# Gaps to the running maxima in an RWKV mixing stage: two VectorE operations replaced by a second key projection and a matmul with a negative identity

## The chip, the cores and the metric

The kernel runs on one core of a Trainium2 chip. The metric is the device time of one execution in microseconds; an execution is launched once and computes the whole decoder layer. The engines are PE (TensorE), DVE (VectorE), ACT (ScalarE), POOL (GpSimd) and SP (SyncE, which only issues DMAs here). "PEld" is the weight load of a matmul.

## The reference

The layer is mixing (RWKV), cross attention, and an attention and mixture-of-experts block. Only the mixing stage changes. Its core, for 16 sequences of 128 steps and 256 channels, once forward and once backward in time:

```
r, k, v = x @ rkv_w.T            # per direction, 256 channels each
per step t, per channel:
    ku = k + u;  m = max(mx, ku)
    y  = (exp(mx-m)*num + exp(ku-m)*v) / (exp(mx-m)*den + exp(ku-m))
    mw = mx + w;  mn = max(mw, k)          # w = -exp(time_decay)
    num = exp(mw-mn)*num + exp(k-mn)*v
    den = exp(mw-mn)*den + exp(k-mn)
    mx  = mn
out = (sigmoid(r) * y) @ out_w.T ;  x = layernorm(x + out)
```

All four exponentials depend only on the difference of the key `k` and the running maximum before it, `mx`: they are `exp(-relu(...))` of plus or minus that difference and a number that is constant in a channel.

## The kernel before

The program is written by hand, engine by engine, with semaphores; no scheduler reorders it. The stages follow one another; the mixing stage runs roughly from 65 to 274 us of the profiled execution.

**Units.** Mixing works on 16 units: 4 groups of 4 sequences, and in each group 4 units of 128 channels (u = 0, 1 forward, u = 2, 3 backward). A unit is 128 partitions by 512 columns (4 sequences of 128 steps). Unit n has place u = n mod 4 in group n // 4. PSUM has three banks for even and three for odd units (receptance, key, value); two more banks hold the output rows of a group.

**What one unit passes through.** PE projects it (`project`, L488: six fp32 128x512 matmuls, which stand in the trace as 12 records). DVE makes the running maxima of the keys with four scans of 128 columns (L655) into `top`, then two gaps with `scalar_tensor_tensor` on the key bank and `top` (L664 and L666) into two of the four planes of `weight`. ACT makes all four planes from these with two Relu passes over 1024 columns (L585, L587), and one Exp over 2048 (L589). POOL multiplies values into them (`new_parts`, L609 and L611). DVE runs the two carry scans (L672, L675). POOL forms numerator and denominator (`add_old`, L620 twice, L623, L624). DVE divides (`finish`, L682, the reciprocal L685, L689) into `y`. After a group's four units PE adds the residual (`copy_rows`, L547, two matmuls) and the output projections (`project_out`, L553, one for each unit), and DVE normalises (`norm`, `norm_rows`).

**The order that is written out.** Step n of DVE is: carry scans of unit n; `gaps` of unit n+2; at u = 3 `norm_rows` of the group before; `finish` of unit n-1; at u = 2 `norm` of the group before. Ahead of `finish` it waits, at u = 1, 2 and 3 of every group but the first, until the output projection of unit n-4-1 has read `y` (`unit_joined` at n-4, L720). Step n of PE is: `project` of unit n+2; at u = 1 `copy_rows` and output projections 0 and 1 of the group before; at u = 2 its output projections 2 and 3. `project` of unit m waits only until unit m-2 has left its banks: values and gates copied by ACT (`vr_ready`) and gaps made by DVE (`gaps_ready`). Step n of ACT is `begin` of unit n+2: gate, values, Relus, Exp. Step n of POOL is `new_parts` of n+1, then `add_old` of n. The last step with a unit to project is n = 13.

**Opening.** The projection of unit 0 and its maxima and gaps lie in the preparation stage. PE's mixing program (`tensor`) begins once the last transposes of that stage have left their banks; POOL and the rest of DVE and ACT begin once SP has signalled the stage.

## Time and profile before

| | us |
|---|---|
| median of 3 runs | 1191.3 (1191.14 to 1192.22) |
| the profiled execution | 1189.91 |
| its span, first to last instruction | 1188.2 |

Over the whole span PE is busy 82%, DVE 81%, ACT 63%, POOL 51%. These are averages over stages with different limits. Within the mixing stage (65 to 250 us) DVE has next to no gaps. The profile gives start and duration of every instruction; in-order engines overlap the tail of one instruction with the head of the next by about 0.1 us, so the distance from start to start is used for what an instruction costs in a row.

### The profile page before, as it was taken

The page shows a single profiled execution, that of the slowest core. Times are in us where ns is not written, and L with a number is a line of the kernel's source. Part 1 is how long each engine was busy: PE and PEld are TensorE (multiplying, and loading weights), DVE is VectorE, ACT ScalarE, POOL GpSimd, SP SyncE. Part 2 cuts the span into 40 slices and gives each one's busy share as a digit, 9 for nine tenths or more (in the row PEclk, how much of TensorE's full clock was granted, in tenths as well). Part 3 has the DMA queues.
Part 4 walks back from the last instruction along what each step waited for, and adds up shares of the span by engine and source line. Part 5 has one row for each costly group of instructions (what it writes and reads, how often), then busy time and mean ns, then how long its engine had stood idle before and what let it go on. Part 6 is the DMA issues. An engine that isn't in the chain of part 4 may idle for free.

```text
span 1188.2 us, 24715 instructions
## 1 busy us (share of the span) xinstructions
PE 968.9 (82%) x7366; PEld 744.4 (63%) x7367; DVE 959.0 (81%) x2172; ACT 752.0 (63%) x1885; POOL 601.8 (51%) x639
## 2 busy tenths in 40 slices
PE   0495877535999989968999999993799999999991
PEld 0342433324777777745666666662799999999990
DVE  6859999997888888876999998866577777777773
ACT  4864444304888888844666777651477777777773
POOL 2859776853444444421557667751544444434333
PEclk9897988867998899988999999996899999999995
DMA  5860010131333333216122112221122222222224
GB/s 192 346 224 3 1 36 1 35 115 59 117 120 120 120 120 120 90 58 249 38 101 71 59 49 72 67 63 38 32 42 44 37 40 40 39 43 38 40 32 151
DMA packets 53493, 96.77 MB, mean 81 GB/s; under 512 B 9840, under 2 KB 41584, under 8 KB 52928
## 3 DMA queue, kind: packets, MB, share of 16 engines
q1 hardware_dynamic: 45328, 83.35, 20.4%
q0 software_dynamic: 8112, 12.78, 6.2%
q8 instruction: 25, 0.41, 0.1%
q14 instruction: 28, 0.23, 0.1%
HBM read 66.37 MB, written 29.74 MB: 81 GB/s over the span
## 4 chain that ended last, share of the span: by engine, by line
PE 43%; DVE 34%; issue 9%; ACT 5%; POOL 4%; DMA 3%; DVEq 0%; SPq 0%; ACTq 0%; POOLq 0%
PE banks L2166 15%; PE banks L2176 10%; DVE mix_sums L685 4%; DVE carry L672 2%; DVE peak L1186 2%; DVE carry L675 2%; PE banks L1452 2%; DVE probs L1189 2%; DVE whole_stat L241 2%; DVE whole_stat L240 2%; PE banks L1430 1%; PE banks L1475 1%; PE banks L1467 1%; ACT whole_level L1075 1%; PE banks L924 1%
## 5 line engine op out<-in xcount | busy, mean ns | idle before, releaser
L2266 DVE SCALAR_TENSOR_TENSOR expert_gate<-banks,expert_steps,expert_chunk 128x128 f32<-128x128 f32 x546 | 164.8, 346 | 76.8 <-ACT expert_chunk L2226 58.2
L2166 PE MATMUL banks<-expert_parts,levels 128*128 128x128 bf16 x3276 | 196.9, 220 | 1.0 <-ACT expert_parts L2221 1.0
L2166 PEld LDWEIGHTS banks<-expert_parts,levels 128*128 x3276 | 189.0, 98 | 6.9 <-issue 1.2
L2230 ACT ACTIVATE silu<-expert_gate,expert_steps 128x128 f32<-128x128 f32 x273 | 109.6, 402 | 77.9 <-DVE expert_gate L2266 76.0
L488 PE MATMUL banks<-x_turned,w_rkv 128*128 128x512 f32 (+1 forms) x192 | 103.1, 698 | 39.4 <-DVE weight L666 35.4
L2176 PE MATMUL banks<-down,up 128*128 x546 | 134.9, 387 | 0.0
L2337 POOL DMA_INDIRECT summed_d<-expert_y,expert_target x39 | 62.5, 1602 | 126.6 <-ACT expert_y L2236 123.5
L2226 ACT COPY expert_chunk<-banks 128x256 f32<-128x256 f32 x273 | 99.8, 366 | 14.5 <-PE banks L2166 12.9
L1151 POOL TENSOR_TENSOR whole<-whole_level,whole_stat 128x896 bf16<-128x896 f32 x32 | 53.2, 1684 | 102.1 <-DVE whole_level L1226 102.1
L2176 PEld LDWEIGHTS banks<-down,up 128*128 128x128 f32 x546 | 97.6, 190 | 10.4 <-issue 0.4
L488 PEld LDWEIGHTS banks<-x_turned,w_rkv 128*128 128x128 f32 x192 | 42.2, 226 | 97.5 <-issue 92.9
L2273 DVE SCALAR_TENSOR_TENSOR up<-expert_gate,expert_steps,silu 128x128 f32<-128x128 f32 x273 | 95.0, 348 | 8.2 <-ACT silu L2230 8.2
L1075 ACT ACTIVATE whole_level<-whole_raw,whole_stat 128x128 f32<-128x128 f32 x224 | 91.2, 486 | 0.2 <-DVE whole_stat L261 0.2
L585 ACT ACTIVATE weight<-weight 128x1024 f32<-128x1024 f32 x16 | 17.0, 1064 | 70.5 <-DVE weight L666 70.4
L962 PE MATMUL banks<-v_ones,probs_t 128*128 128x17 f32 x512 | 61.1, 261 | 0.0
L962 PEld LDWEIGHTS banks<-v_ones,probs_t 128*128 128x128 f32 x512 | 59.7, 192 | 0.0
L1430 PE MATMUL banks<-attend_w,xn_t 128*128 128x512 f32 x128 | 58.7, 601 | 0.0
L1475 PE MATMUL banks<-attend_w,o_turn 128*128 128x256 f32 x256 | 58.1, 380 | 0.5 <-ACT logits L1591 0.5
L2309 POOL DMA_INDIRECT expert_rows<-normed_d,token x39 | 41.2, 1057 | 31.3 <-POOL token L2306 30.5
L1570 ACT ACTIVATE att_probs<-att_probs,low_peak 128x128 f32<-128x128 f32 x128 | 49.5, 390 | 11.4 <-DVE low_peak L1816 11.3
L1699 POOL TENSOR_TENSOR att_probs<-att_probs,att_share 128x1024 f32<-128x1024 f32 x16 | 30.3, 1896 | 49.8 <-DVE att_share L1820 49.8
L685 DVE RECIPROCAL mix_sums<-gate 128x512 f32<-128x512 f32 x16 | 53.6, 3353 | 0.6
(265 smaller groups left out, 2421.4 us busy)
## 6 DMA issues: line engine op xcount, KB each, us to landing
whole_raw<-in_weight_jobs SPq DMA_DIRECT2D x16, 896.0 KB, 5.3
levels_d<-whole_t SPq DMA_DIRECT2D x16, 448.0 KB, 2.8
levels<-levels_d SPq DMA_DIRECT2D x16, 448.0 KB, 3.9
raw<-in_weight_jobs SPq DMA_DIRECT2D x6, 896.0 KB, 4.9
numbers_d<-turned SPq DMA_DIRECT2D x6, 896.0 KB, 7.4
down<-in_weight_jobs SPq DMA_DIRECT2D x5, 896.0 KB, 7.1
normed_d<-normed_parts SPq DMA_DIRECT2D x16, 192.0 KB, 1.9
attend_w<-numbers_d SPq DMA_DIRECT2D x3, 896.0 KB, 6.6
```

The lines of the kernel that those rows point to most:

```text
L488: last = pe.matmul(banks[:, 3 * (u % 2) + m, :], w_rkv[:, kc, col:col + P], x_turned[d][:, kc, bass.ds(g * GT, GT)], start=(kc == 0), stop ...
L685: st.did(dve.reciprocal(sums[p][:, 1, :], gate[u][:, :]))
L962: last = pe.matmul(banks[:, HEADS, head * (XK + 1):(head + 1) * (XK + 1)], probs_t[h][:, 4 * m + a, :], v_ones[j][:, head, :], start=True, ...
L1075: last = act.activation(level[j][:, a, :], raw[j][:, a, :], ACT.Identity, bias=stat[j][:, BIAS, a:a + 1], scale=stat[j][:, INV, a:a + 1])
L1430: last = pe.matmul(banks[:, at[m], :], xn_t[:, c, :], w_qkv[:, c, 512 * m:512 * m + 512], start=(c == 0), stop=(c == DC - 1))
L1475: last = pe.matmul(banks[:, TURN, 0:D], o_turn[:, h, :], w_o[:, h, :], start=(h == 0), stop=(h == QH - 1))
L2166: last = pe.matmul(banks[:, at, (m * DC + c) * ROWS:(m * DC + c + 1) * ROWS], levels[:, bass.ds(expert * (2 * JOB) + (m * JOB + (f * DC + ...
L2176: last = pe.matmul(banks[:, Y + j, 0:D], up[j][:, f, :], down[:, bass.ds(expert * JOB + f * D, D)], start=(f == 0), stop=(f == FC - 1))
L2226: act.copy(chunk[slot(j, f)][:, :, :], halves(at)[:, :, 0, :]).then_inc(chunk_ready, 1)
L2230: act.activation(silu[slot(j, f)][:, :], gate[slot(j, f)][:, 0, :], ACT.Silu, scale=steps[j][:, 0, 0, f:f + 1]).then_inc(silu_ready, 1)
L2266: last = dve.scalar_tensor_tensor(out=gate[slot(j, f)][:, m, :], in0=halves(at)[:, m, 1, :], scalar=steps[j][:, m, 1, f:f + 1], in1=chunk[ ...
L2273: dve.scalar_tensor_tensor(out=up[j][:, f, :], in0=gate[slot(j, f)][:, 1, :], scalar=steps[j][:, 1, 0, f:f + 1], in1=silu[slot(j, f)][:, : ...
```

## The change

The two gap operations of DVE go. After the maxima of a unit are there, PE writes the key bank again: it projects the keys a second time (two matmuls) and adds, with a third matmul, `top` times a negative identity. The bank then holds key minus maximum. ACT reads that bank four times, with a Relu each that has the channel's constant as bias and +1 or -1 as scale, and the Exp stays. The reuse of the banks now hangs on ACT's fourth Relu (`gaps_read`), which also takes the place of `vr_ready` and `decay_ready`. Three small operations on DVE at the opening make the negated constants and the negative identity. The step of PE becomes: `project` of n+2, `gap` of n+2, then what it had at u = 1 and u = 2. The diff, cut to its core:

```diff
-    EDGES, INNER = slice(0, 4, 3), slice(1, 3)
 def project(pe, g, u, n, wait=True):
         if wait:
-            pe.wait_ge(vr_ready, n - 1)
-            pe.wait_ge(gaps_ready, n - 1)
+            pe.wait_ge(gaps_read, DECAY + n - 1)
...
+        def gap(g, u, n):
+            d, c, p = u // DC, u % DC, u % 2
+            col = (3 * d + 1) * D + c * P
+            pe.wait_ge(tops_ready, n + 1)
+            for kc in range(DC):
+                pe.matmul(banks[:, 3 * p + 1, :], w_rkv[:, kc, col:col + P], x_turned[d][:, kc, bass.ds(g * GT, GT)],
+                          start=(kc == 0), stop=False)
+            pe.matmul(banks[:, 3 * p + 1, :].rearrange("p (b s) -> p b s", b=GB), minus_ident[:, :], top[p][:, :, 0:S],
+                      start=False, stop=True).then_inc(gaps_ready, 1)
...
             if u < 2 or not is_last:
                 project(pe, g + (u + 2) // UNITS, (u + 2) % UNITS, n + 2)
+                gap(g + (u + 2) // UNITS, (u + 2) % UNITS, n + 2)
...
+        gap(0, 0, 0)
         project(pe, 0, 1, 1, False)
+        gap(0, 1, 1)
         in_groups(step, pe)
...
         def soften(u, n):
             act.wait_ge(gaps_ready, n + 1)
-            w = weight[u]
-            st.did(act.activation(w[:, INNER, :], w[:, EDGES, :], ACT.Relu))
-            st.wait()
-            st.did(act.activation(w[:, EDGES, :], w[:, EDGES, :], ACT.Relu, scale=-1.0))
-            st.wait()
+            if not (isinstance(n, int) and n == 0):
+                act.wait_ge(sums_ready, n + 1)
+            w, over = weight[u], banks[:, 3 * (u % 2) + 1, :]
+            act.activation(w[:, FROM_PAST, :], over, ACT.Relu, bias=exp_decay[:, u:u + 1])
+            act.activation(w[:, FROM_NEW, :], over, ACT.Relu, bias=step_decay[:, u:u + 1], scale=-1.0)
+            act.activation(w[:, OLD, :], over, ACT.Relu, bias=first[:, u:u + 1])
+            act.activation(w[:, NOW, :], over, ACT.Relu, bias=minus_first[:, u:u + 1], scale=-1.0).then_inc(gaps_read, 1)
+            act.wait_ge(gaps_read, DECAY + n + 1)
             act.activation(w[:, :, :], w[:, :, :], ACT.Exp, scale=-1.0).then_inc(weights_ready, 1)
...
-        def gaps(u, n):
+        def tops(u, n):
             p = u % 2
             dve.wait_ge(rkv_ready, n + 1)
+            if not isinstance(n, int) or n > 1:
+                dve.wait_ge(gaps_ready, n - 1)
             key = banks[:, 3 * p + 1, :]
             for b in range(GB):
                 last = dve.tensor_tensor_scan(top[p][:, b, 1:S + 1], step_decay[:, u:u + 1].to_broadcast([P, S]),
                                               key[:, b * S:(b + 1) * S], LOWEST, ALU.add, ALU.max)
-            st.did(last)
-            st.wait()
-            if not (isinstance(n, int) and n == 0):
-                dve.wait_ge(sums_ready, n + 1)
-            before = top[p][:, :, 0:S]
-            keys = key.rearrange("p (b s) -> p b s", b=GB)
-            past, now = (weight[u][:, m, :].rearrange("p (b s) -> p b s", b=GB) for m in (FROM_PAST, NOW))
-            dve.scalar_tensor_tensor(out=past, in0=before, scalar=step_decay[:, u:u + 1], in1=keys,
-                                     op0=ALU.add, op1=ALU.subtract)
-            dve.scalar_tensor_tensor(out=now, in0=keys, scalar=first[:, u:u + 1], in1=before,
-                                     op0=ALU.add, op1=ALU.subtract).then_inc(gaps_ready, 1)
+            last.then_inc(tops_ready, 1)
...
-        dve.wait_ge(decay_ready, 1)
-        st.did(dve.tensor_scalar(step_decay[:, :], step_decay[:, :], -1.0, None, ALU.mult))
+        dve.wait_ge(gaps_read, DECAY)
+        dve.tensor_scalar(minus_first[:, :], first[:, :], -1.0, None, ALU.mult)
+        dve.tensor_scalar(minus_ident[:, :], k.ident, -1.0, None, ALU.mult)
+        st.did(dve.tensor_scalar(step_decay[:, :], exp_decay[:, :], -1.0, None, ALU.mult))
```

How it moves the instructions. First PE in the group loop, from the projection of step u = 0 to the first output projections of step u = 1, before (`x_turned,w_rkv` is the projection, `x_group,consts` the residual, `w_out,y` an output projection):

```order
L488 MATMUL banks<-x_turned,w_rkv 128x512 x5
L483 REGISTER_ALU
L488 MATMUL banks<-x_turned,w_rkv 128x512 x6
L544 ISA
L547 MATMUL banks<-x_group,consts 128x512 x2
L553 MATMUL banks<-w_out,y 128x256 x8
L483 REGISTER_ALU
```

The same place now; L491 is the projection, L550 and L552 are the gap (the second key projection and `top` times the negative identity), L560 the residual, L566 the output projections:

```order
L491 MATMUL banks<-x_turned,w_rkv 128x512 x6
L548 REGISTER_ALU
L550 MATMUL banks<-x_turned,w_rkv 128x512 x2
L552 MATMUL banks<-top,minus_ident 128x512
L557 ISA
L560 MATMUL banks<-x_group,consts 128x512 x2
L564 REGISTER_ALU
L566 MATMUL banks<-w_out,y 128x256 x8
L491 ISA
```

A gap, which waits for DVE's scans of its unit, stands between every projection and what follows it.

DVE in the group loop, step u = 2, from the second carry scan to the division of the unit before (`top` are the maxima, `gate<-gate,mix_sums` opens `finish`), before:

```order
L675 SCALAR_TENSOR_TENSOR carry<-weight,new_value 128x512
L655 SCALAR_TENSOR_TENSOR top<-step_decay,banks 128x128 x4
L74 REGISTER_ALU
L664 SCALAR_TENSOR_TENSOR weight<-top,step_decay,banks 128x512
L666 SCALAR_TENSOR_TENSOR weight<-banks,first,top 128x512
L720 REGISTER_ALU
L681 REGISTER_ALU
L682 SCALAR_TENSOR_TENSOR gate<-gate,mix_sums 128x512
```

And now:

```order
L682 SCALAR_TENSOR_TENSOR carry<-weight,new_value 128x512
L672 SCALAR_TENSOR_TENSOR top<-step_decay,banks 128x128 x4
L727 REGISTER_ALU
L688 REGISTER_ALU
L689 SCALAR_TENSOR_TENSOR gate<-gate,mix_sums 128x512
```

The two gap operations are gone and nothing else on DVE has moved; the division follows the maxima directly.

## Rows read from the trace of the kernel before

**Rows 1.** Waits from 60 to 240 us: who waited for whom; us, times, longest.
```profile
ACT weight L585 <- DVE weight L666: 70.4, 14, 5.9
PE banks L488 <- DVE weight L666: 35.4, 9, 7.6
```

**Rows 2.** Timeline of DVE over one unit: start us, duration us, then the instruction.
```profile
132.92 2.29 DVE L672 TENSOR_TENSOR_SCAN carry<-weight 128x512 f32<-128x512 f32 x1
...
135.13 2.22 DVE L675 TENSOR_TENSOR_SCAN carry<-weight,new_value 128x512 f32<-128x512 f32 x1
...
137.27 1.32 DVE L655 TENSOR_TENSOR_SCAN top<-step_decay,banks 128x128 f32<-128x128 f32 x4
...
138.63 0.75 DVE L664 SCALAR_TENSOR_TENSOR weight<-top,step_decay,banks 128x512 f32<-128x512 f32 x1
...
139.96 0.68 DVE L682 SCALAR_TENSOR_TENSOR gate<-gate,mix_sums 128x512 f32<-128x512 f32 x1
...
144.67 2.29 DVE L672 TENSOR_TENSOR_SCAN carry<-weight 128x512 f32<-128x512 f32 x1
...
149.02 1.32 DVE L655 TENSOR_TENSOR_SCAN top<-step_decay,banks 128x128 f32<-128x128 f32 x4
```

**Rows 3.** Timeline of PE: start us, duration us, instruction, idle before in brackets.
```profile
70.08 26.02 PE L488 MATMUL banks<-x_turned,w_rkv 128*128 128x512 f32 x60 [1.51 <-ACT turned L369]
...
140.19 6.98 PE L488 MATMUL banks<-x_turned,w_rkv 128*128 x12 [2.77 <-DVE weight L666]
...
170.56 1.88 PE L547 MATMUL banks<-x_group,consts 128*128 128x512 f32 x4
172.28 3.62 PE L553 MATMUL banks<-w_out,y 128*128 128x256 f32 x16
```

**Rows 4.** Timeline of DVE at the opening.
```profile
75.54 1.35 DVE L655 TENSOR_TENSOR_SCAN top<-step_decay,banks 128x128 f32<-128x128 f32 x4 [0.79 <-PE banks L488]
...
100.69 1.32 DVE L655 TENSOR_TENSOR_SCAN top<-step_decay,banks 128x128 f32<-128x128 f32 x4
```

**Rows 5.** Timeline of DVE where POOL leaves the carry scans alone.
```profile
158.47 1.22 DVE L672 TENSOR_TENSOR_SCAN carry<-weight 128x512 f32<-128x512 f32 x1
159.60 1.20 DVE L675 TENSOR_TENSOR_SCAN carry<-weight,new_value 128x512 f32<-128x512 f32 x1
160.72 1.33 DVE L655 TENSOR_TENSOR_SCAN top<-step_decay,banks 128x128 f32<-128x128 f32 x4
...
173.40 1.32 DVE L655 TENSOR_TENSOR_SCAN top<-step_decay,banks 128x128 f32<-128x128 f32 x4
```

**Rows 6.** Timeline of ACT and POOL: steps on the way to the weights.
```profile
50.48 5.50 ACT L356 ACTIVATE level<-raw,stat 128x128 f32<-128x128 f32 x14 [0.48 <-DVE stat L261]
...
133.09 0.60 ACT L497 ACTIVATE gate<-banks 128x512 f32<-128x512 f32 x1 [0.69 <-DVE y L689]
133.59 0.58 ACT L500 COPY values<-banks 128x512 f32<-128x512 f32 x1
...
142.25 1.91 ACT L589 ACTIVATE weight<-weight 128x2048 f32<-128x2048 f32 x1
...
144.32 1.56 POOL L609 TENSOR_TENSOR new_value<-weight,values 128x512 f32<-128x512 f32 x1 [1.33 <-ACT weight L589]
```

**Rows 7.** Timeline of DVE at the end of the stage.
```profile
233.13 1.32 DVE L655 TENSOR_TENSOR_SCAN top<-step_decay,banks 128x128 f32<-128x128 f32 x4
...
235.81 0.68 DVE L682 SCALAR_TENSOR_TENSOR gate<-gate,mix_sums 128x512 f32<-128x512 f32 x1
...
240.52 2.28 DVE L672 TENSOR_TENSOR_SCAN carry<-weight 128x512 f32<-128x512 f32 x1
...
244.86 0.66 DVE L682 SCALAR_TENSOR_TENSOR gate<-gate,mix_sums 128x512 f32<-128x512 f32 x1
```

**Rows 8.** PE in stretches: length, busy us, granted clock, DMA.
```profile
139.00:139.50 0.50, 0.00 (x0) 1.00 0.00 0
140.00:140.50 0.50, 0.31 (x1) 0.50 0.00 0
```

More of the change, by code:

```diff
@@ L156, in __init__ @@
         self.x_group = self.buffer(self.mix_inputs, "x_group", [GB, D])
+        self.exp_decay = self.buffer(self.mix_inputs, "exp_decay", [UNITS])
         self.step_decay = self.buffer(self.mix_inputs, "step_decay", [UNITS])
+        self.minus_first = self.buffer(self.mix_inputs, "minus_first", [UNITS])
+        self.minus_ident = self.buffer(self.mix_inputs, "minus_ident", [P])
         self.top_keys = [self.buffer(self.mix_inputs, f"top{p}", [GB, S + 1]) for p in range(2)]
@@ L429, in mix_stage @@
     LOADS, FIRST_LOADS = 5, 4
+    DECAY = 1
     with ExitStack() as own:
         step_decay, top = k.step_decay, k.top_keys
+        exp_decay, minus_first, minus_ident = k.exp_decay, k.minus_first, k.minus_ident
         weight = k.unit_weight + [k.buffer(own, f"weight{u}", [4, GT]) for u in range(2, UNITS)]
@@ L443, in mix_stage @@
     k.mix_inputs.close()
-    decay_ready = k.semaphore("decay_ready")
     rkv_ready = k.semaphore("rkv_ready")
-    vr_ready = k.semaphore("vr_ready")
+    tops_ready = k.semaphore("tops_ready")
     gaps_ready = k.semaphore("gaps_ready")
+    gaps_read = k.semaphore("gaps_read")
     weights_ready = k.semaphore("weights_ready")
@@ L499, in take_gate @@
             act.wait_ge(new_ready, 2 * n + 2)
-        act.copy(values[p][:, :], banks[:, 3 * p + 2, :]).then_inc(vr_ready, 1)
+        act.copy(values[p][:, :], banks[:, 3 * p + 2, :])
     def open_decay(act):
         act.wait_ge(k.mix_loads, 16 * LOADS)
-        act.activation(step_decay[:, :], decay[:, :], ACT.Exp).then_inc(decay_ready, 1)
+        act.activation(exp_decay[:, :], decay[:, :], ACT.Exp).then_inc(gaps_read, DECAY)
     def open_gate(act):
@@ L575, in scalar @@
     def scalar(act):
-        st = k.steps["act"]
         def begin(u, n):
@@ L597, in scalar @@
         begin(1, 1)
-        st.done(1, 4)
-        in_groups(step, act, st, 2 * UNITS)
-        st.done(1, st.at)
+        in_groups(step, act)
     def gpsimd(pool):
@@ L715, in step @@
             if u < 2 or not is_last:
-                gaps((u + 2) % UNITS, n + 2)
+                tops((u + 2) % UNITS, n + 2)
             if u == 3 and not is_first:
@@ L731, in vector @@
         dve.sem_inc(mix_normed, 1)
-        dve.wait_ge(decay_ready, 1)
-        st.did(dve.tensor_scalar(step_decay[:, :], step_decay[:, :], -1.0, None, ALU.mult))
+        dve.wait_ge(gaps_read, DECAY)
+        dve.tensor_scalar(minus_first[:, :], first[:, :], -1.0, None, ALU.mult)
+        dve.tensor_scalar(minus_ident[:, :], k.ident, -1.0, None, ALU.mult)
+        st.did(dve.tensor_scalar(step_decay[:, :], exp_decay[:, :], -1.0, None, ALU.mult))
         st.wait()
-        gaps(0, 0)
+        tops(0, 0)
         dve.wait_ge(k.begun, k.begins["mix"])
@@ L738, in vector @@
             st.did(dve.memset(carry[p][:, :, 0:1], 0.0))
-        gaps(1, 1)
+        tops(1, 1)
         st.done(1, st.at)
-        in_groups(step, dve, st, 3 * UNITS + 2)
+        in_groups(step, dve, st, 2 * UNITS + 2)
         finish(UNITS - 1, N - 1)
```

## The prediction

> **What bounds the kernel now.** I read the waits of the mixing stage first. PE and ACT both wait for DVE's second gap operation, PE nine times for 35.4 us in all and ACT 14 times for 70.4 us [rows 1], so PE and ACT have slack and DVE leads. The timeline of DVE says the same: a unit goes from one set of maxima at 137.27 to the next at 149.02, 11.75 us, and each instruction starts as the last ends [rows 2]. Three things are to be seen in that unit. The gap operations take 139.96 - 138.63 = 1.33 us. The division and what goes with it (L682 to L689) takes 144.67 - 139.96 = 4.7 us. The two carry scans take 137.27 - 132.92 = 4.35 us, but only 160.72 - 158.47 = 2.25 us where POOL is not at work [rows 5]. So some 2.1 us of a unit is time in which POOL blocks DVE. PE projects a unit in 26.02 / 5 = 5.2 us at full clock (60 records, 12 a unit) [rows 3], and may do so up to two units ahead of DVE, because nothing of a unit on PE depends on DVE's maxima.
>
> **What is removed.** DVE loses 1.33 us in each unit. The cover of everything else matters more than that gain, so I follow the marks at which DVE starts the maxima of a unit; "maxima of 4" is that mark for unit 4.
>
> **What is added on PE.** A gap is three matmuls of the shape of which a projection has six: 5.2 / 2 = 2.6 us. Fifteen of them, after the first, come to 39 us of PE work in a stage in which PE had time; the work alone costs nothing. Its place does. PE works in order, and a gap waits for the maxima of its unit; the projection of the next unit stands behind it. PE can no longer run ahead. From one mark to the next there is now a chain through both engines: the maxima 1.36 us (138.63 - 137.27), a signal of 0.16 us (DVE's last gap operation ended at 140.03, between 139.96 and PE's start at 140.19) [rows 2, 3], the gap 2.6, the next projection 5.2, and 0.26 us from PE's last record to DVE (70.08 + 5.2 = 75.28 against the start of the maxima at 75.54) [rows 3, 4]. That is 9.6 us. Where output projections stand between gap and projection it is longer.
>
> **The opening.** Before, PE projected five units in one piece from 70.08 on [rows 3], and DVE found every projection ready but the first. Now the gap of unit 0 stands in front of the projection of unit 1, so the maxima of 1 start at 75.54 + 2.6 = 78.1; then three links of 9.6 give the maxima of 4 at 106.9, against 100.69 before [rows 4]: **+6.2 us**. The three small new operations of DVE fall in the preparation stage; the maxima of 0 have until 70.08, where PE may take the first gap, and I cost them at nothing. If that cover went, they would cost what they run over, at most a few us.
>
> **The three units after it.** The maxima of 4 to those of 7 took 137.27 - 100.69 = 36.6 us [rows 2, 4]. An interval that DVE sets is now between 9.6 us (the chain) and 11.75 - 1.33 = 10.4 us (all blocking stays). POOL's blocking may fall, since the weights come later (below) and its work moves behind the carry scans. I take 10.0 us, the middle. Three intervals take 30.0: **-6.6 us**. At the maxima of 7 the two kernels are level (-0.4).
>
> **A group in the loop.** Four intervals, each set by what is late there.
> - From the maxima taken in step u = 1: PE has gap, residual and two output projections before the next projection. DVE has a wait of its own: `finish` may overwrite `y` of place 0 only after that unit's output projection, which was done long before and now stands behind the gap. The residual costs 172.28 - 170.56 = 1.7 us and an output projection 1.75 (half of 16 records, 3.6 with the tail) [rows 3]. DVE: 1.36 + 0.16 + 2.6 + 1.7 + 1.75 + 0.26 = 7.85 us until `finish` may begin, then 4.7, then the carry scans 2.25 (POOL has had time to finish): 14.8. PE: 1.36 + 0.16 + 2.6 + 1.7 + 3.5 + 5.2 + 0.26 = 14.8 also. Before it was 11.75.
> - From those of u = 2: gap, two output projections, projection: 1.36 + 0.16 + 2.6 + 3.5 + 5.2 + 0.26 = 13.1. The norm of DVE fits beside it. Before: 160.72 - 149.02 = 11.7 [rows 2, 5].
> - From those of u = 3, with `norm_rows`: 173.40 - 160.72 = 12.7 before [rows 5]; now at most 12.7 - 1.33 = 11.4, and 10.2 with no blocking left. I take 11.0.
> - From those of u = 0: 10.0, as above.
>
> The sum is 48.9 us. Two groups, the maxima of 7 to those of 15, take 97.8 against 233.13 - 137.27 = 95.9 [rows 2, 7]: **+1.9 us**.
>
> **The end.** Step n = 13 is again a step u = 1. `finish` began 235.81 - 233.13 = 2.7 us after the maxima began [rows 7]; now it waits for the output projection, 7.85 us: +5.2. POOL has meanwhile made the products of the last units, so the next two carry scans, 244.86 - 240.52 = 4.3 us before [rows 7], take 2.25: -2.1. Together **+3.1 us**. All later work starts from the end of this stage, so the sum is passed on whole.
>
> **ACT.** The two Relu passes over SBUF become four over the bank. A pass of 512 columns from a bank takes 0.50 us (133.59 - 133.09); one of 128 columns with bias and scale from a buffer takes 5.5 / 14 = 0.39 [rows 6], so a bias may cost up to 0.3 more. Four take 2.0 to 3.2 us; I take 2.7 against about 2.2 before. From the end of the maxima to the end of the Exp is then 0.16 + 2.6 + 0.26 + 2.7 + 1.9 = 7.6 us, against 142.25 + 1.91 - 138.63 = 5.5. POOL, which waited 1.33 us for the Exp [rows 6], gets weights 2.1 us later; but DVE scans with them a whole unit later, which covers that.
>
> Sum: +6.2 - 6.6 + 1.9 + 3.1 = **+4.6 us**. It is made against the profiled execution: 1189.9 us, of which 1188.2 is span, becomes 1194.5. The median of the runs lies 1.4 us above that execution, so the forecast is 1191.3 + 4.6 = **1195.9 us**.
>
> **A rule against a row.** The rows show a carry scan of 1.2 us taking 2.29 us beside POOL [rows 2, 5]. The Trainium skill (SBUF — State Buffer, "Who interferes with whom") says why: VectorE instructions with two SBUF inputs and GpSimd instructions hold one port pair exclusively, each for its whole length. The trace agrees in size: the loss of 1.1 us is about one POOL operation. By that rule blocking can't simply go away when DVE has less other work. That makes the rival "port" below.
>
> **Rivals.**
> *Faster.* The chain is shorter than I think, or DVE's wait at u = 1 is not last, and DVE sets the pace throughout: 14 units times 1.33 = 18.6 us less, some given back at the opening: 1175 to 1187. For it: DVE is the bound and PE has 35.4 us of waits. Against it: the written order, which no duration changes. It needs residual and output projections (5.2 us) to be hidden from the chain. 0.12.
> *No change.* Blocking goes nearly altogether and the seven intervals that I put at 10.0 and 11.0 sit on the chain at 9.6 and 10.2: 5 x 0.4 + 2 x 0.8 = 3.6 us less, +1.0: 1192.3. For it: POOL's products fall after DVE's scans if the weights are late. 0.20.
> *Port.* In a unit POOL has six operations of about 1.2 us, and DVE four with two inputs from SBUF (two scans of 1.1, two of 0.65): 7.3 + 3.5 = 10.8 us if no two overlap. Seven intervals are 0.8 longer: 1195.9 + 5.6 = 1201.5. Against it: the unit before had such overlap and blocking in 11.75 us with POOL idle for 1.3 us. 0.10.
> *Clock.* At 139 us the granted clock was 1.00 and PE idle, at 140 it was 0.50 (1.2 GHz), and the projection took 6.98 instead of 5.2 us [rows 3, 8]. PE now idles 1.5 to 3 us per unit before each gap. Each fall puts 1.8 us on a chain that has no slack; three to five falls give 1201 to 1205. For it: it happened after 2.77 us of idling. Against it: PE is busier now. 0.10.
> That the change does not do what it says is excluded: L664 and L666 are gone from DVE's row of instructions.
>
> **Chances.** Forecast as it stands, 1194 to 1200: 0.48. With port and clock that makes slower 0.68; no change (within 0.2%, 2.4 us, about what a measurement of this kernel can tell) 0.20; faster 0.12. The range, 1190 to 1204 us, reaches into no change and over most of clock and port.
>
> **What would show it.** Right: the maxima of 4 near 106.9, with DVE waiting some 5 us for PE's projection in each of the first units; intervals of 14 to 15 and 13 us at u = 1 and 2, the first with DVE's L689 waiting for PE; carry scans mostly at 1.2 us; PE waiting for L672. Wrong: DVE without gaps in the loop (faster), or half clock on PE in many units (clock).

## The result

| | before | after |
|---|---|---|
| median, us | 1191.56 (1191.14 to 1192.22, 4 runs) | 1203.66 (1201.23 to 1205.20, 4 runs) |
| ratio, 95% interval | 1 | 1.0097 (1.0084 to 1.0109) |
| the profiled execution | 1189.91 | 1205.20 |
| its span | 1188.2 | 1203.4 |

The change makes the kernel 12.1 us slower, where 4.6 were forecast. The time lies in the range of 1190 to 1204 us, but only 0.34 us below its upper end, and outside the 1194 to 1200 us of the forecast as it stands. Between the two profiled executions there are 15.3 us, because the one of after lies 1.5 us above its median and the one of before 1.7 below. The last operation of the mixing stage, the normalised output, starts 12.7 us later (284.01 instead of 271.34), and 2.5 us more lie in stages that the change doesn't touch. From that operation to the end the profiled executions take 916.9 us before, 919.4 after, and 918.1 to 922.4 in the nine experiments below; why is not shown.

### The profile page after: what moved, and what is told of

Read it like the earlier page. It is cut to its first block, busy times and chain, and to the rows that moved or that the text cites. A ratio compares the mean times of both kernels' runs of the same rounds, so it can differ in the third digit from the quotient of the medians.

```text
span 1203.4 us, 24891 instructions
## 1 busy us (share of the span) xinstructions
PE 1004.0 (83%) x7462; PEld 759.7 (63%) x7463; DVE 930.5 (77%) x2142; ACT 755.1 (63%) x1917; POOL 591.3 (49%) x639
## 4 chain that ended last, share of the span: by engine, by line
PE 52%; DVE 29%; issue 8%; ACT 6%; POOL 3%; DMA 2%; DVEq 0%; ACTq 0%; POOLq 0%; SPq 0%
PE banks L2175 15%; PE banks L2185 10%; PE banks L491 4%; DVE mix_sums L692 3%; PE banks L550 2%; DVE peak L1195 2%; PE banks L1461 2%; DVE whole_stat L243 2%; DVE probs L1198 2%; ACT whole_level L1084 2%; DVE whole_stat L244 2%; PE banks L933 1%; PE banks L1439 1%; PE banks L1476 1%; DVE top L672 1%
## 5 line engine op out<-in xcount | busy, mean ns | idle before, releaser
L2185 PEld LDWEIGHTS banks<-down,up 128*128 128x128 f32 x546 | 97.6, 190 | 10.4 <-issue 0.4
L491 PE MATMUL banks<-x_turned,w_rkv 128*128 128x512 f32 (+1 forms) x192 | 88.3, 611 | 2.4 <-ACT turned L372 2.4
L491 PEld LDWEIGHTS banks<-x_turned,w_rkv 128*128 128x128 f32 x192 | 38.2, 200 | 50.1 <-issue 47.1
L550 PE MATMUL banks<-x_turned,w_rkv 128*128 128x512 f32 (+1 forms) x64 | 36.1, 691 | 30.9 <-DVE top L672 28.9
L1579 ACT ACTIVATE att_probs<-att_probs,low_peak 128x128 f32<-128x128 f32 x128 | 49.5, 390 | 11.2 <-DVE low_peak L1825 11.1
L692 DVE RECIPROCAL mix_sums<-gate 128x512 f32<-128x512 f32 x16 | 53.6, 3353 | 0.6
```

Source lines behind the costliest of these rows:

```text
L491: last = pe.matmul(banks[:, 3 * (u % 2) + m, :], w_rkv[:, kc, col:col + P], x_turned[d][:, kc, bass.ds(g * GT, GT)], start=(kc == 0), stop ...
L692: st.did(dve.reciprocal(sums[p][:, 1, :], gate[u][:, :]))
L2185: last = pe.matmul(banks[:, Y + j, 0:D], up[j][:, f, :], down[:, bass.ds(expert * JOB + f * D, D)], start=(f == 0), stop=(f == FC - 1))
```

## The profile after

In the new kernel `project` is L491, the second key projection of a gap L550 and its negative identity L552, the residual L560, the output projections L566, the Relus L601 to L604, the Exp L606, the maxima L672, the carry scans L679 and L682, and the division L689, L692 and L696. First the waits from 60 to 260 us (who waited for whom; us in all, times, longest), which answer to [rows 1]:

```profile
ACT weight L601 <- PE banks L552: 65.2, 16, 8.2
...
POOL new_value L624 <- ACT weight L606: 45.5, 14, 11.5
...
PE banks L550 <- DVE top L672: 28.9, 15, 3.8
DVE top L672 <- PE banks L491: 25.6, 9, 5.5
DVE gate L689 <- PE banks L566: 19.3, 3, 6.5
```

Before, everybody waited for DVE. Now PE waits for DVE at every gap, and DVE waits for PE in return: 9 times for a projection and 3 times for an output projection. Neither leads; they take turns. In the page's chain of work that ended last, PE's share of the whole span rose from 43% to 52%, and DVE's fell from 34% to 29%.

The timeline of PE at the opening (start, duration, instruction, idle time before it) answers to the first of [rows 3]. Where 60 records of projections stood in one piece, there is now a pattern of 9.44 us, with PE idle for 1.45 us in each:

```profile
80.47 1.99 PE L550 MATMUL banks<-x_turned,w_rkv 128*128 128x512 f32 x4 [1.45 <-DVE top L672]
82.30 1.02 PE L552 MATMUL banks<-top,minus_ident 128*128 128x512 f32 x2
83.15 5.31 PE L491 MATMUL banks<-x_turned,w_rkv 128*128 128x512 f32 x12
89.91 1.98 PE L550 MATMUL banks<-x_turned,w_rkv 128*128 128x512 f32 x4 [1.45 <-DVE top L672]
```

DVE at the same links, and then in the first unit where it is late itself (answers to [rows 2, 4]). Its wait for PE is in brackets; there is none at 118.92:

```profile
97.94 1.35 DVE L672 TENSOR_TENSOR_SCAN top<-step_decay,banks 128x128 f32<-128x128 f32 x4 [4.44 <-PE banks L491]
...
107.62 1.32 DVE L672 TENSOR_TENSOR_SCAN top<-step_decay,banks 128x128 f32<-128x128 f32 x4
108.87 1.66 DVE L689 SCALAR_TENSOR_TENSOR gate<-gate,mix_sums 128x512 f32<-128x512 f32 x1
...
114.56 2.30 DVE L679 TENSOR_TENSOR_SCAN carry<-weight 128x512 f32<-128x512 f32 x1
116.78 2.22 DVE L682 TENSOR_TENSOR_SCAN carry<-weight,new_value 128x512 f32<-128x512 f32 x1
118.92 1.32 DVE L672 TENSOR_TENSOR_SCAN top<-step_decay,banks 128x128 f32<-128x128 f32 x4
```

L689 takes 1.66 us here. In [rows 2] the same operation takes 0.68. POOL is at work at that moment (its L626 runs from 108.72 to 109.98).

The loop at u = 1. DVE has its maxima at 139.69 and then stands still for 6.47 us, until PE has done gap, residual and one output projection; PE goes on with the second output projection and the next projection:

```profile
147.48 0.69 DVE L689 SCALAR_TENSOR_TENSOR gate<-gate,mix_sums 128x512 f32<-128x512 f32 x1 [6.47 <-PE banks L566]
...
154.45 1.33 DVE L672 TENSOR_TENSOR_SCAN top<-step_decay,banks 128x128 f32<-128x128 f32 x4
```

```profile
142.89 1.02 PE L552 MATMUL banks<-top,minus_ident 128*128 128x512 f32 x2
143.75 1.88 PE L560 MATMUL banks<-x_group,consts 128*128 128x512 f32 x4
145.46 3.62 PE L566 MATMUL banks<-w_out,y 128*128 128x256 f32 x16
148.92 5.31 PE L491 MATMUL banks<-x_turned,w_rkv 128*128 x12
155.84 1.98 PE L550 MATMUL banks<-x_turned,w_rkv 128*128 x4 [1.61 <-DVE top L672]
```

At three gaps (120.30, 180.48, 232.19) PE had idled longer, for 3.30, 3.76 and 3.76 us. There the gap took about twice its time:

```profile
180.48 3.78 PE L550 MATMUL banks<-x_turned,w_rkv 128*128 x4 [3.76 <-DVE top L672]
184.05 1.91 PE L552 MATMUL banks<-top,minus_ident 128*128 128x512 f32 x2
185.76 5.57 PE L491 MATMUL banks<-x_turned,w_rkv 128*128 x12
192.78 1.98 PE L550 MATMUL banks<-x_turned,w_rkv 128*128 x4 [1.45 <-DVE top L672]
```

The stretches around it (length, PE, weight load, DVE, ACT, POOL, then the granted clock) give the reason: 0.94 while PE idled, 0.50 (1.2 GHz) during the gap. At the third fall the clock was down while PE was still idle:

```profile
179.00:179.50 0.50, 0.00 (x0) 0.00 (x0) 0.50 (x3) 0.00 (x0) 0.50 (x1) 0.94 0.00 0
181.00:181.50 0.50, 0.50 (x2) 0.01 (x1) 0.50 (x1) 0.00 (x0) 0.50 (x2) 0.50 0.00 0
231.00:231.50 0.50, 0.00 (x0) 0.00 (x0) 0.50 (x3) 0.00 (x0) 0.50 (x1) 0.50 0.00 0
```

The end of the stage, which answers to [rows 7]:

```profile
242.82 1.35 DVE L672 TENSOR_TENSOR_SCAN top<-step_decay,banks 128x128 f32<-128x128 f32 x4 [2.75 <-PE banks L491]
250.56 0.69 DVE L689 SCALAR_TENSOR_TENSOR gate<-gate,mix_sums 128x512 f32<-128x512 f32 x1 [6.38 <-PE banks L566]
```

All intervals between two maxima, read from the starts of the maxima in the timeline of DVE:

| maxima of | before | predicted | after |
|---|---|---|---|
| 0 to 4, in all | 35.6 | 41.8 | 41.6 |
| 4 to 5, 5 to 6, 6 to 7 | 12.7, 12.1, 11.75 | 10.0 each | 11.3, 11.1, 9.7 |
| 7 to 8 and 11 to 12 (u = 1) | 11.75, 11.75 | 14.8 | 14.8, 14.8 |
| 8 to 9 and 12 to 13 (u = 2) | 11.7, 11.7 | 13.1 | 12.9, 12.9 |
| 9 to 10 and 13 to 14 (u = 3) | 12.7, 12.8 | 11.0 | 11.8, 11.8 |
| 10 to 11 and 14 to 15 (u = 0) | 11.75, 11.75 | 10.0 | 12.3, 12.0 |

## The experiments

The theory: the time comes from the written order. The gap waits for DVE's maxima, and what stands behind it on PE (the next projection, output projections) waits with it. The rivals: the half clock, DVE's port shared with POOL, and the later weights. Three kernels change what is computed: e3, e4 and e5 leave out the gap, so that ACT takes its Relus from the bare key bank and the maxima are not subtracted; e4, and later e8, also leave out POOL's multiplications of the old sums. The versions are compared with before in the same series of runs (medians 1192.87 for e1 to e4, 1194.08 for e5 to e7, 1192.38 for e8 and e9). "After" would stand at 1.0097 times these: 1204.4, 1205.7 and 1203.9.

### e1: keep PE busy ahead of the three slow gaps

```diff
         last.then_inc(rkv_ready, 1)      # at the end of project
+        # ahead of it, in step u = 3 of the first group and u = 0 of the others:
+        for kc in range(DC):
+            last = pe.matmul(banks[:, 3 * (u % 2) + 2, :], ...)   # the value projection once more
```

> The changed kernel, with the two matmuls of the value projection done twice in the projections of units 4 to 6, 10 and 14, where PE idled 3.3 to 3.8 us before the next gap (120.30, 180.48 and 232.19 us in the trace after). It adds 1.7 us of PE work a time and computes nothing new. Clock theory (each of the three idle stretches makes the granted clock fall and lengthens the gap and the projection behind it by about 1.9 to 2.6 us, all of it on the chain): PE stays at full clock through the group loop, the intervals that were 11.1, 12.3 and 12.0 us fall to about 9.7 to 10, and the time falls by 4 to 6 us. Rival (the clock falls elsewhere or the lost time is DVE's own): the 1.7 us of PE work are added to chains without slack and the time is the same or up to 2 us more.

Measured: 1200.45 us, ratio 1.0065 (1.0044 to 1.0086), some 4 us less than after. PE's gap that answers to the one at 180.48 of after (timeline of PE):

```profile
179.25 1.98 PE L554 MATMUL banks<-x_turned,w_rkv 128*128 x4 [2.06 <-DVE top L676]
181.07 1.02 PE L556 MATMUL banks<-top,minus_ident 128*128 128x512 f32 x2
```

PE idled 2.06 instead of 3.76 us, the gap ran at full clock, and the interval from the maxima of 10 to those of 11 fell from 12.3 to 9.4, which is the bare chain. From 14 to 15 it fell only to 11.1, since the clock fell there all the same (the gap at 228.11 took 2.87 us after 2.05 us of idling). From 5 to 6 it stayed at 11.1, but not because the clock fell. The edit reaches two steps in this place and four in all (units 5, 6, 10 and 14). The repeat in the projection of unit 5 (L495 at 115.77) cured the slow gap, which took 1.98 us at 119.24. The one in the projection of unit 6 (at 127.07), which no slow gap called for, stands on the chain and costs the 1.7 us again. So the falls are a real part of the loss: about 2.8, 2.6 and 1.7 us above the chain's 9.44.

### e2: PE projects one unit more ahead of each gap

```diff
+            project(pe, ..., n + 3)          # u < 1 or not the last group
             if u == 1 and not is_first: ...  # residual, output projections
             if u == 2 and not is_first: ...
-            project(pe, ..., n + 2)          # stood ahead of the output projections
             gap(..., n + 2)                  # now behind them
...
         gap(0, 1, 1)
+        project(pe, 0, 2, 2)                 # ahead of the loop
```

> The changed kernel with PE one unit further ahead: step n of PE projects unit n+3, then does the output projections, and only then the gap of unit n+2. Same instructions. Chain theory (the order on PE, project of n+3 and the output projections behind gap n+2, costs the opening 7 us, the intervals of 14.8 and 12.9 us in each group, and the wait of the division at the end 5 us): DVE no longer waits for PE in the group loop, every interval is set by DVE at about 11.3 us, plus 1.8 and 2.0 us a group for the norm, and the time comes to between 1188 and 1192 us. Rival (PE's 39 us of additional work are what costs, or the later weights): the time stays above 1198 us.

Measured: 1209.12 us, ratio 1.0135 (1.0114 to 1.0155), 5 us slower than after. A miss. The bank of unit n + 3 is that of n + 1, and its key bank is free only when ACT has read the gap of n + 1. The waits show what came in place of the old one:

```profile
PE banks L491 <- ACT weight L606: 30.7, 12, 2.6
...
DVE gate L691 <- PE banks L566: 15.9, 2, 8.0
```

From gap over Relus and projection to the next gap the chain is now closed without DVE: 10.5 us at u = 0, and 16.4 and 14.5 where output projections stand in it. With two banks for the key, a bank that is written twice can't be projected a unit further ahead as a whole.

### e3: no gap at all

```diff
-                gap(g + (u + 2) // UNITS, (u + 2) % UNITS, n + 2)
...
-            act.wait_ge(gaps_ready, n + 1)
+            act.wait_ge(tops_ready, n + 1)
...
-            if not isinstance(n, int) or n > 1:
-                dve.wait_ge(gaps_ready, n - 1)     # DVE, ahead of the maxima
```

> The changed kernel without the three matmuls of the gap: ACT reads the bare keys as soon as the maxima are done, so the maxima are never subtracted and the mixing weights are others. It shows what DVE and POOL do when neither gap operations nor PE's chain is there. If removing the two gap operations were worth their 1.33 us, DVE's interval in the loop would be 10.4 us or less and the mixing stage 15 to 19 us shorter than before: 1173 to 1177 us. Port theory (DVE's gap operations read a PSUM bank and left POOL undisturbed; without them more of DVE's two-input operations fall into POOL's, as in the interval of 11.3 us from 107.62 to 118.92 in the trace after, with 3.0 us of blocking against 2.1 before): the interval is 10.8 to 11.3 us and the time 1180 to 1186 us.

Measured: 1179.53 us, ratio 0.9886 (0.9861 to 0.9911), 25 us less than after and 13.3 less than before. It is what the removal of the two DVE operations is worth with nothing in their place: the rival "faster" had 1175 to 1187. DVE in one unit (timeline):

```profile
110.46 1.32 DVE L656 TENSOR_TENSOR_SCAN top<-step_decay,banks 128x128 f32<-128x128 f32 x4
111.70 0.66 DVE L673 SCALAR_TENSOR_TENSOR gate<-gate,mix_sums 128x512 f32<-128x512 f32 x1
...
116.42 2.10 DVE L663 TENSOR_TENSOR_SCAN carry<-weight 128x512 f32<-128x512 f32 x1
118.45 2.22 DVE L666 TENSOR_TENSOR_SCAN carry<-weight,new_value 128x512 f32<-128x512 f32 x1
120.59 1.32 DVE L656 TENSOR_TENSOR_SCAN top<-step_decay,banks 128x128 f32<-128x128 f32 x4
```

The interval is 10.1 us here and in the three others from the maxima of 4 to those of 8, below the 10.4 that I had given as the upper end with all blocking kept, and below the 10.8 of the rival "port". Both scans are blocked as in [rows 2], and L673 is not. In these units blocking did not grow. It did later: from the maxima of 10 to those of 11 L673 takes 1.68 us (at 165.96) with both scans blocked, and the interval is 11.3, as in after, though there is neither gap nor wait for PE. Over the eleven intervals from the maxima of 4 to those of 15 e3 takes 119.6 us where before takes 132.4. That is 1.17 us a unit, of the 1.33 removed. The time lies between the two ranges of the expectation.

### e4: e3 with four POOL operations instead of six

```diff
-            for m in range(2):
-                last = pool.tensor_tensor(sums[p][:, m, :], weight[u][:, OLD, :], carry[p][:, m, 0:GT], ALU.mult)
...
+            st.did(pool.tensor_tensor(sums[p][:, 1, :], carry[p][:, 1, 0:GT], weight[u][:, NOW, :], ALU.add))
...
+            pool.tensor_tensor(sums[p][:, 0, :], carry[p][:, 0, 0:GT], new_value[p][:, 1, :], ALU.add).then_inc(sums_ready, 1)
```

> As the kernel without the gap matmuls, and POOL leaves out the two multiplications by the weight of the old state in the numerator and the denominator (6 POOL operations of 1.2 us a unit become 4; it adds the carry itself). DVE's instructions are the same. Port theory: blocking falls, by up to the 2.4 us a unit that POOL no longer holds the port, towards DVE's unblocked 8.3 us a unit; interval 8.5 to 9.5 us, the time 15 to 30 us below that of the kernel without gap matmuls. Rival (DVE's instructions are just that long in this place): interval as in the kernel without gap matmuls, within 0.3 us.

Measured: 1175.50 us, ratio 0.9860 (0.9841 to 0.9880), 4.0 less than e3. Expected were 15 to 30 less, a miss. The intervals from the maxima of 4 on are 10.4 to 11.2 (one is 9.4), where e3 has 10.1 to 12.5. So with 2.4 us less of POOL in a unit some are longer than in e3: 10.9 instead of 10.1 from 4 to 5. Two sets of scans that follow each other in the timeline of DVE:

```profile
126.07 2.28 DVE L660 TENSOR_TENSOR_SCAN carry<-weight 128x512 f32<-128x512 f32 x1
128.28 1.19 DVE L663 TENSOR_TENSOR_SCAN carry<-weight,new_value 128x512 f32<-128x512 f32 x1
...
135.52 2.29 DVE L660 TENSOR_TENSOR_SCAN carry<-weight 128x512 f32<-128x512 f32 x1
137.73 2.22 DVE L663 TENSOR_TENSOR_SCAN carry<-weight,new_value 128x512 f32<-128x512 f32 x1
```

The sum of port time does not set the interval. By these rows, what counts is which of DVE's operations with two inputs from SBUF has a POOL operation beside it.

### e5: e3 with weights 1.9 us later

```diff
+            act.activation(w[:, :, :], w[:, :, :], ACT.Relu).then_inc(relus_done, 1)   # all four planes again
+            act.wait_ge(relus_done, n + 1)
             act.activation(w[:, :, :], w[:, :, :], ACT.Exp, scale=-1.0)
```

> As the kernel without the gap matmuls, with one more Relu pass of ACT over the four planes ahead of the Exp. It changes no value; the weights come 1.9 us later. DVE's and POOL's instructions are the same. Phase theory (what a unit costs DVE is decided by which POOL operation each of its four two-input operations meets, and later weights shift POOL against DVE): the intervals in the loop move from 10.1 and 10.5 us towards the 11.3 us of the changed kernel, and the time by +5 to +15 us. Rival (the weights are early enough, and only PE's chain and the clock made the changed kernel slow): intervals within 0.2 us of the kernel without gap matmuls, the time within 3 us.

Measured: 1179.50 us, ratio 0.9881 (0.9865 to 0.9896), the same as e3. Weights that come 1.9 us later than in e3 cost nothing. In some units the blocking moved: L676 takes 1.66 us and the first scan 1.22, and the interval is 10.2 (175.89 to 186.11) all the same. In the loop the Exp ends 7.66 us after the maxima begin, where it is 5.72 in e3, 6.89 before and 8.65 in after. So a delay beyond that of before costs nothing here; e5 doesn't reach the last 1.0 us of after. e7 does: its Exp ends 8.6 us or more after the maxima begin, and it is 18 us faster than after. Late weights are thus not what makes the new kernel slow.

### e6: output projections ahead of projection and gap

```diff
-            project(...n + 2); gap(...n + 2)     # stood ahead of both ifs
             if u == 1 and not is_first: ...      # residual, output projections 0, 1
             if u == 2 and not is_first: ...      # output projections 2, 3
+            project(...n + 2); gap(...n + 2)
```

> The changed kernel with the residual and the output projections of the group before moved ahead of projection and gap in PE's steps u = 1 and u = 2. Same instructions. Chain theory: they stay between two gaps, so the long intervals (14.8 and 12.9 us) stay and only move one place forward; DVE's wait of 6.4 us ahead of the division at u = 1 goes, which in the loop was no longer than PE's own chain, and at the end of the stage was on the path alone: 5 to 6 us less. Rival (DVE's wait at u = 1 was what made the 14.8 us): that interval falls to 12 us or less in each group, 8 to 10 us less in all.

Measured: 1204.10 us, ratio 1.0089 (1.0072 to 1.0106), 1.6 us less than after, which is less than the two intervals can tell apart. Expected were 5 to 6, a miss. The long intervals moved forward by one unit (14.6 us from the maxima of 6 and of 10, 12.9 from those of 7 and 11). DVE's wait at the division is gone at the end, but a third long interval came up, since in the last group, too, two output projections (of the group before) now lie ahead of a projection for which DVE waits:

```profile
230.31 1.35 DVE L672 TENSOR_TENSOR_SCAN top<-step_decay,banks 128x128 f32<-128x128 f32 x4 [0.40 <-PE banks L491]
...
244.92 1.35 DVE L672 TENSOR_TENSOR_SCAN top<-step_decay,banks 128x128 f32<-128x128 f32 x4 [4.74 <-PE banks L491]
```

The chain through both engines is as long wherever the output projections stand, as long as they lie between one gap and the next projection.

### e7: the order that the chain asks for

PE projects receptance and value of unit n + 3 (whose banks are free early, after ACT's copies), then the output projections, then only the key of n + 3, then the gap of n + 2.

```diff
+            project(pe, ..., n + 3, parts=(0, 2))   # waits for vr_ready, ACT's two copies
             if u == 1 and not is_first: ...
             if u == 2 and not is_first: ...
+            project(pe, ..., n + 3, parts=(1,))     # waits for gaps_read
             gap(..., n + 2)
...
         gap(0, 1, 1)
+        project(pe, 0, 2, 2)                        # ahead of the loop
```

> The changed kernel with PE a unit further ahead, but with the receptance and value projections of unit n+3 and the output projections ahead of the wait for ACT's Relus of unit n+1, and only its key projection behind that wait; then the gap of unit n+2. Same instructions. The run with PE further ahead showed PE waiting 2.5 us for ACT's Relus in each unit, so that gap, Relus and projection made a new chain of 10.6 us and longer with output projections; here 3.5 us of projection cover that wait. Theory: DVE no longer waits for PE in the loop; intervals of 10.1 to 11.3 us plus the norm, no wait of the division, 1180 to 1187 us, below the kernel before. Rival (the 39 us of PE work or the later weights cost as such): above 1190 us.

Measured: 1187.42 us, ratio 0.9943 (0.9928 to 0.9957): 18 us less than after, and 6.7 less than before (the medians), so it beats both. From the maxima of 5 on, DVE sets the pace again in several units:

```profile
117.69 1.32 DVE L679 TENSOR_TENSOR_SCAN top<-step_decay,banks 128x128 f32<-128x128 f32 x4
118.94 0.66 DVE L696 SCALAR_TENSOR_TENSOR gate<-gate,mix_sums 128x512 f32<-128x512 f32 x1
...
123.64 2.11 DVE L686 TENSOR_TENSOR_SCAN carry<-weight 128x512 f32<-128x512 f32 x1
...
127.81 1.32 DVE L679 TENSOR_TENSOR_SCAN top<-step_decay,banks 128x128 f32<-128x128 f32 x4
```

The pattern is that of e3. The expectation did not hold in full. Intervals of the loop go up to 12.7 us, DVE waited once for an output projection (3.32 us ahead of the division at 186.07), and the time lies 0.4 us above the 1180 to 1187 us. All arithmetic of the changed kernel is kept here, the gap matmuls and the four Relus included; only the order on PE differs, and one signal. Of the 25 us between after and e3, this gives back 18.

### e8: the changed kernel with four POOL operations

The same edit in POOL as in e4, now in the changed kernel.

> The changed kernel, but POOL leaves out the two multiplications of the old sums by the weight OLD (the sums come out differently), so a unit has four POOL operations instead of six. Theory (POOL blocks DVE's first division step L689, which now follows the maxima directly, and the carry scans): the intervals of 11.3 and 11.8 us between two sets of maxima fall to 9.7 to 10.4, L689 takes 0.7 us in them, those of 14.8 and 12.9 stay, because both engines' written order sets them; 5 to 7 intervals of 1 us less give 4 to 8 us: 1196 to 1200 us. Rival (these intervals are set by the order on PE and the low clock, blocking is only slack filled up): intervals as before within 0.3 us, 1202 to 1205 us.

Measured: 1200.91 us, ratio 1.0065 (1.0040 to 1.0090), 3 us less than after; 4 to 8 were expected, and the 95% intervals of the two just touch. At the opening the theory holds in the main. The intervals from the maxima of 4 on are 9.4, 9.4, 9.4 instead of 11.3, 11.1, 9.7, and the scans take 1.2 us. The division (L686) is still hindered, 1.05 to 1.54 us where 0.7 was expected, but DVE has time for that, since it waits for PE again:

```profile
106.34 1.35 DVE L669 TENSOR_TENSOR_SCAN top<-step_decay,banks 128x128 f32<-128x128 f32 x4 [0.74 <-PE banks L491]
107.61 1.05 DVE L686 SCALAR_TENSOR_TENSOR gate<-gate,mix_sums 128x512 f32<-128x512 f32 x1
```

In the loop it does not. At u = 3 the interval is 12.1 and 13.1 us (11.8 after), with L686 at 1.70 and the second scan at 2.22 us, and in the longer one the first scan at 2.28 as well: POOL's work came to lie on them. And behind such an interval PE has idled longer, and the clock falls:

```profile
175.77 3.78 PE L550 MATMUL banks<-x_turned,w_rkv 128*128 x4 [4.05 <-DVE top L669]
```

### e9: e7 with repeated matmuls where PE idled

The repeated value projection of e1, in e7's first part of the projection, ahead of the three gaps that ran slowly there (PE had idled 3.83, 4.11 and 4.41 us), and in one step more (n = 4).

> The version with PE a unit further ahead and the projection split round the output projections (1187.4 us), and in addition the four matmuls of the value projection are repeated in the three steps ahead of which PE idled 3.8 to 4.4 us and its clock fell (gap matmuls of 3.78 instead of 1.98 us at 119.07 and 173.61, of 3.38 at 220.42). Clock theory: PE idles about 2.1 to 2.7 us there, the clock stays at 1.0 and the gap ends 1.9 to 2.6 us earlier, of which DVE, which leads in this version, gets only a part: 2 to 4 us less, 1183 to 1186 us. Rival (DVE sets the pace throughout, PE's low clock lies beside it): the same within 1 us, 1186 to 1188 us.

Measured: 1188.34 us, ratio 0.9958 (0.9943 to 0.9973), the same as e7. Two of the three gaps ran at full clock and nothing was gained: where DVE leads, PE's half clock lies beside its work. The rival was right. In the timeline of PE one more thing is to be seen:

```profile
174.00 3.68 PE L556 MATMUL banks<-x_turned,w_rkv 128*128 x4 [2.67 <-DVE top L683]
...
219.91 1.98 PE L556 MATMUL banks<-x_turned,w_rkv 128*128 128x512 f32 x4 [2.70 <-DVE top L683]
```

After idle times of 2.67 and 2.70 us, both behind a whole projection with the repeat, the clock had fallen once and once not. The idle time just ahead doesn't tell alone whether the clock falls.

## Why the prediction was right, and where not

The direction and the mechanism were right, the size was short by 7.5 us of the 12.1 measured. That the time still lies in the range is in part luck. The range reached to 1204 for the sake of the clock and port rivals, each held at 0.10, and the median ended 0.34 us inside it. The clock rival had 1201 to 1205 for three to five falls and came out by the number, but the three falls that came make up 5.4 us of the 8.1 that the sum missed; most of the rest is POOL's blocking. Term by term, in the two profiled executions:

| term | predicted | measured |
|---|---|---|
| opening, to the maxima of 4 | +6.2 | +6.9 |
| maxima of 4 to 7 | -6.6 | -4.5 |
| two groups of the loop | +1.9 | +7.3 |
| end of the stage | +3.1 | +3.0 |
| sum | +4.6 | +12.7 |

**The opening: right.** The links are 9.44 us, with 9.6 in the sum. The maxima of 4 start at 107.62; 106.9 was forecast. Of the 6.9, 1.0 us comes from ahead of the stage: the maxima of 0 start at 66.06 instead of 65.10. In the experiments they start anywhere from 63.54 (e7) to 66.07 (e6), in e1 and e8, whose instructions are the same up to there, at 65.0. So this looks like scatter, not like the change.

**The loop at u = 1 and 2, and the end: right.** 14.76 and 12.87 us stand against 14.8 and 13.1. DVE waits at L689 for the output projection, as written. At the end L689 starts 7.74 us behind the maxima (7.85 in the sum), and the two carry scans take 257.53 - 255.28 = 2.25. ACT's four Relus start 0.56 to 0.59 us apart (111.88, 112.47, 113.03, 113.60, and the Exp at 114.33): 2.45 us, with 2.7 in the sum. e3 and e7 show that the chain is the cause: without it, or with the order that loosens it, 25 and 18 us are gone. e7 is the stricter of the two, since it keeps every matmul and still has three slow gaps.

**The first failed step: "An interval that DVE sets is now between 9.6 us (the chain) and 11.75 - 1.33 = 10.4 us (all blocking stays)."** The upper end is no upper end. It was read from the one unit of [rows 2], where L682 takes 0.68 us. The units right after the opening were not like it. The 36.6 us that the sum itself had for three of them are 12.2 a unit. Taking 1.33 off each gives -4.0; the sum booked -6.6, and -4.5 was measured. In the interval from 4 to 5 the kernel before already had its first division step blocked, behind the two gap operations as well, beside POOL's L611 (103.20 to 104.46). The timeline of DVE, before:

```profile
103.38 1.64 DVE L682 SCALAR_TENSOR_TENSOR gate<-gate,mix_sums 128x512 f32<-128x512 f32 x1
```

That interval was 12.7 us, so 11.4 without the gap operations, and 11.3 was measured: scans and L689 lose 1.1 + 1.0 + 1.0 = 3.1 us. Here blocking stayed, and the sum had taken it to fall. At u = 3 it is new: the step took 0.69 us before (at 165.22) and takes 1.42 now, with the second scan at 2.22, and the interval is 11.8 instead of the 11.0 of the sum. Together this makes +1.3 once and +0.8 twice, 2.9 us. e8 shows the cause in the opening, where with less of POOL the same intervals fall to 9.44. e4 and e8 together show that the total of POOL's work does not price it; which operation meets which does, as far as the rows tell.

The rule that the prediction weighed (the Trainium skill, SBUF — State Buffer, "Who interferes with whom": VectorE instructions with two SBUF inputs and GpSimd instructions shut each other out, each for its whole length) agrees with such rows: a scan takes 1.20 or 2.22 us and L689 0.69 or 1.66, and values between them (a scan of 1.58, L689 of 1.03 to 1.42) fit a POOL operation that was already on its way. The rival's sum didn't come out: e3 has an interval of 10.1 where "no two overlap" gave 10.8. The rows show where some of the difference went. In e3's unit scans and POOL operations alternate and end at 117.45, 118.52, 119.59, 120.67 and 121.73, 1.06 to 1.08 us apart, where the sum has 1.1 for a scan and 1.2 for a POOL operation. POOL's work beside the reciprocal (L612 and the first of L621, from 113.45 on, beside 112.40 to 115.75) runs at its full pace of 1.2 us.

**The second failed step: the clock was a rival at 0.10 and should have been in the sum.** "PE now idles 1.5 to 3 us per unit before each gap" was true for the chain's intervals (1.45 to 1.66 us, and 2.04 ahead of the first gap; the clock held at all of them). But an interval that DVE sets at 11.3 or 11.8 leaves PE idle for 3.3 to 3.8 us, and [rows 3, 8] already had a fall after 2.77. Three falls came. They cost 1.7, 2.8 and 2.6 us above the chain of 9.44, or 1.1, 2.3 and 2.0 above the 10.0 of the sum: 5.4 us in all. "Each fall puts 1.8 us on a chain" was short as well, because three matmuls of the gap and the start of the projection run at half speed. Together they are 7 us above the chain. e1 gave back 4 of them: one fall is gone without a price, another cost less, and the gain of the third was taken up by the repeat in unit 6.

The two steps add 2.9 + 5.4 = 8.3 us. The interval from 6 to 7 (9.7) and the two at u = 2 were 0.8 us shorter than forecast in all, and the opening was 0.7 longer; that leaves 8.2, against the 8.1 by which the sum missed the 12.7. The two steps also hang together: POOL's blocking lengthens one interval, PE idles in it, and the fall lengthens the next. In e8, where the interval from 4 to 5 is 9.44 us, no gap of the opening is slow. A sum that prices each alone, with a middle value for the one and a small chance for the other, misses that.

**What stays open.** Why POOL's operations meet L689 in one unit and the scans in the next was read from timelines, not predicted by anything. e7 still lies some 7 us (by the ratios) above e3, which leaves out the gap. In the two profiled executions, from the maxima of 0 to the stage's last operation, e7's stage is even 12.6 us longer (203.6 against 191.0); it begins 2.4 us earlier there, and its later stages take 3.8 us less. The opening has the largest part, 7.3 us: the maxima of 0 to those of 4 take 41.7 us (14.0, 9.4, 5.1, 13.1), where e3 has 34.4 (10.4, 5.1, 5.2, 13.7), with the first gaps of PE between the projections. The eleven intervals after it have 3.4, the end 2.0. No version was run with another opening.

## What to carry to other kernels

When work moves from the leading engine to one with slack, price its place in that engine's order before its duration: 2.6 us of PE work a unit were cheap (e7, which keeps them, took 3.4 us more than e3 over eleven intervals of the loop), but a wait for DVE's newest result, ahead of work that DVE needs next, turned two engines that ran side by side into one chain. Split the later work by what it really waits for (here: receptance and value early, only the key late), put the waiting piece last, and the same arithmetic is 1.5% faster (e7 against after). Look for idle stretches of PE that the new order makes: here every gap behind 2.89 us of idling or more ran slowly, and where PE was on the chain a fall cost 1.7 to 2.8 us. And take the blocking of a unit from the rows of that unit, not from those of another.

## What the runs showed of the hardware

- TensorE's clock in this stage, over the gaps of after and of e1, e6, e7, e8 and e9: it held at every gap ahead of which PE had idled 1.67 us or less. It went both ways between 2.04 and 2.70 us: gaps of 1.98 us after 2.04 (after, e6), 2.06 (e1), 2.13 and 2.70 (e9), but of 2.87 after 2.05 (e1) and 3.68 after 2.67 (e9). At all eleven with 2.89 us or more the gap was slow, 2.71 to 3.78 us instead of 1.98 for its first part.
- A Relu of 512 columns from a PSUM bank with a bias from a buffer takes 0.57 us start to start, 0.07 more than the gate's pass over a bank (0.50, [rows 6]). I had allowed up to 0.3.
- One DVE operation with two SBUF inputs can lose as much as 1.0 us (0.69 to 1.66, once 1.82 in e7) beside a POOL operation of 1.26 us; a scan loses up to 1.1. A POOL operation beside them also grows, from 1.26 to 2.17 us. With a third of POOL's operations gone (e4 against e3), the intervals that DVE sets were partly shorter (9.4) and partly longer (10.9 instead of 10.1).
